# Splitting the value products of an fp32 attention into 64-row halves: four accumulator banks, scan units of 512 and a normalisation that goes through memory

## The reference

```python
# layer 0, for each image; w1 is 16 x 256
f = w1 @ xf + b1                       # 16 x N
energy = f.T @ f                       # N x N
attention = softmax(energy, axis=-1)
x2 = x + 0.1 * (xf @ attention.T)      # 256 x N
# layer 1: 3x3 convolution of sign(x2) with sign weights times a scale per channel,
# batch normalisation over all images, plus x2
```

## Time and profile before

| | |
|---|---|
| runs | 2257.96 us median of 3 (2257.39 to 2259.11) |
| profiled execution | 2258.62 us, its span 2256.8 us |
| granted TensorE clock, mean | 0.973 |
| busy PE, DVE, ACT, POOL | 95%, 71%, 59%, 36% |
| attention, about 85 to 2035 us | 512 groups |
| before it | projections and the first 24 scan units |
| after it | convolution to about 2203 us, then the final pass |

### The profile page before, as it was taken

The page is one execution under the profiler, slowest core; times in us unless marked ns, Lnnn a source line. Parts: engine busy times, 40 slices in busy tenths (PEclk is TensorE's granted clock), DMA queues, the critical chain, the costliest instruction groups (busy, mean ns, idle before and its releaser), DMA issues. The chain is left out here.

```text
span 2256.8 us, 26470 instructions
## 1 busy us (share of the span) xinstructions
PE 2145.6 (95%) x9152; PEld 1388.8 (62%) x9152; DVE 1613.0 (71%) x1719; ACT 1324.5 (59%) x1789; POOL 806.9 (36%) x664
## 2 busy tenths in 40 slices
PE   5799999999999999999999999999999999999990
PEld 2366666666666666666666666666666666664440
DVE  4677777777677777777677777777777777646778
ACT  3565566666656665666666566666666666652326
POOL 2433223334533333335433333335333333046760
PEclk7799999999999999999999999999999999999995
DMA  4110010011111100012111100011000001116008
GB/s 157 41 42 15 31 42 23 23 49 47 64 42 41 41 23 20 17 43 64 46 42 40 41 23 23 23 59 60 23 23 22 15 15 71 69 68 233 0 33 339
DMA packets 48632, 117.91 MB, mean 52 GB/s; under 512 B 6144, under 2 KB 7040, under 8 KB 48000
## 3 DMA queue, kind: packets, MB, share of 16 engines
q1 hardware_dynamic: 48512, 116.35, 14.8%
HBM read 76.22 MB, written 33.55 MB: 49 GB/s over the span
## 5 line engine op out<-in xcount | busy, mean ns | idle before, releaser
L520 DVE TENSOR_TENSOR Pl<-P,Ph 128x1024 fp32r<-128x1024 f32 x512 | 697.7, 1363 | 407.4 <-POOL Ph L635 359.8
L635 POOL CAST Ph<-P 128x1024 fp32r<-128x1024 f32 x480 | 503.8, 1050 | 1174.8 <-ACT P L434 1174.8
L347 PE MATMUL acc<-Ph,xh 128*128 128x512 f32 x2048 | 875.7, 428 | 0.0
L347 PE MATMUL acc<-Ph,xl 128*128 128x512 f32 x2048 | 805.8, 393 | 0.0
L434 ACT ACTIVATE P<-ee 128x1024 f32<-128x1024 f32 x512 | 525.1, 1026 | 420.1 <-PE ee L333 418.9
L444 ACT ACTIVATE sc<-sc,nb 128x1024 f32<-128x1024 f32 x512 | 557.5, 1089 | 255.9 <-DVE nb L510 255.2
L510 DVE TENSOR_REDUCE nb<-sc 128x1 f32<-128x1024 f32 x512 | 623.8, 1220 | 116.4 <-PE sc L341 116.0
L347 PE MATMUL acc<-Pl,xh 128*128 128x512 f32 x2048 | 637.1, 392 | 0.3
L347 PEld LDWEIGHTS acc<-Ph,xh 128*128 128x128 f32 x2048 | 385.2, 188 | 265.7 <-issue 195.4
L347 PEld LDWEIGHTS acc<-Pl,xh 128*128 128x128 f32 x2048 | 385.7, 188 | 88.5 <-DVE Pl L520 1.2
L347 PEld LDWEIGHTS acc<-Ph,xl 128*128 128x128 f32 x2048 | 386.6, 189 | 68.1 <-issue 5.7
(11 more groups left out here) (100 smaller groups left out, 823.5 us busy)
## 6 DMA issues: line engine op xcount, KB each, us to landing
wk<-xt SPq DMA_DIRECT2D x32, 512.0 KB, 3.6
xres<-x SPq DMA_DIRECT2D x32, 512.0 KB, 3.7
x<-xres SPq DMA_DIRECT2D x32, 512.0 KB, 2.7
xn<-x SPq DMA_DIRECT2D x16, 512.0 KB, 11.9
xr<-x SPq DMA_DIRECT2D x16, 512.0 KB, 10.2
out<-xr SPq DMA_DIRECT2D x16, 512.0 KB, 3.4
An<-x SPq DMA_DIRECT2D x14, 512.0 KB, 5.3
Bn<-x SPq DMA_DIRECT2D x12, 512.0 KB, 5.6
```

What stands on the lines that cost most here:

```text
L347: return pe.matmul(acc[c][:], w[:, m, c * 128:(c + 1) * 128], p[:, s, k * QC:(k + 1) * QC], start=first, stop=last)
L520: nc.vector.tensor_tensor(Pl[:, e % RP, :], P[:, e % 2, :], Ph[:, e % RP, :].bitcast(F32), ALU.subtract).then_inc(pl_done, 1)
L635: nc.gpsimd.tensor_copy(Ph[:, e % RP, :], P[:, e % 2, :]).then_inc(ph_done, 1)
```

## The change

1. Each attend becomes two matmuls of 64 rows, partitions 64 to 127 (`bot`) and 0 to 63 (`top`), into separate accumulators `acc_b[c]` and `acc_t[c]`: four banks in place of two.
2. `sc` shrinks to two tiles of one bank. Scan units are 512 wide, two per group (`SU` = 32 per tile), and a bank is reused one group later. Both scan units and both energies still stand together at the head.
3. VectorE's order becomes maximum, `lower(e - 1)`, maximum: `lower` is one group later and between the two maxima. ScalarE sums after each.
4. The transposition and spreading on TensorE go. VectorE transposes 32 x 32 blocks, SP issues four transfers into `U`, four into a buffer in memory, and one that loads it spread over all partitions into `R` (`load_r`, g = 4).
5. At the end of a tile ScalarE copies the bottom accumulator to `tb` and VectorE scales the top one; GpSimd's `add_x` is now a multiply, an add and an add for each c.
6. The rounding of xh for images 1 to 3 moves from ScalarE to GpSimd. `store_x2` moves from g = 3 to g = 4, and the exponential of the row statistics from g = 8 to g = 9.

```diff
+        acc_t = [ps(f"acct_{c}", [128, QC]) for c in range(CT)]
+        acc_b = [ps(f"accb_{c}", [128, QC]) for c in range(CT)]
-        sc = [ps(f"sc_{k}", [128, GW]) for k in range(2)]
+        sc = [ps(f"sc_{k}", [128, 512]) for k in range(2)]
...
+            def load_r(t):
+                sp.wait_ge(rd_out, 64 * (t + 1))
+                if t >= 1:
+                    sp.wait_ge(top_done, CT * t)
+                    sp.wait_ge(scaled, CT * t)
+                sp.dma_start(R[:], rd.rearrange("(o n) -> o n", o=1).to_broadcast([128, QC])).then_inc(r_in, 16)
...
+            def scan(v):
+                t, w = divmod(v, SU)
+                j, i = divmod(w, QT)
+                if v >= 2:
+                    pe.wait_ge(bsum_done, v - 1)
+                pe.matmul(sc[v % 2][:], U[t % 2][S0:S0 + KE, i * 128:(i + 1) * 128],
+                          T[t // CH % 2][S0:S0 + KE, j * 512:(j + 1) * 512], start=True, stop=True).then_inc(s_done, 1)
...
+            def attend(t, g, c, i, half):
+                k, w, p = ((0, xh, Ph), (0, xl, Ph), (1, xh, Ph), (1, xl, Ph), (0, xh, Pl), (1, xh, Pl))[i]
                 s = (t * G + g) % RP
+                rows = slice(half * 64, (half + 1) * 64)
+                to = (acc_t, acc_b)[half][c]
+                return pe.matmul(to[:], w[rows, g * GM + k, c * 128:(c + 1) * 128], p[rows, s, k * QC:(k + 1) * QC],
+                                 start=g == 0 and i == 0, stop=g == G - 1 and i == 5)
...
+                if 0 <= e < NG:
+                    energy(e, 0)
+                if u < NG:
+                    scan(2 * u)
+                if 0 <= e < NG:
+                    energy(e, 1).then_inc(e_done, 1)
+                if u < NG:
+                    scan(2 * u + 1)
...
+                        for i in range(6):
+                            if c == 0 and i == 4:
+                                pe.wait_ge(pl_done, n + 1)
+                            bot = attend(t, g, c, i, 1)
+                            top = attend(t, g, c, i, 0)
...
+                if g == 0 and t >= 1:
+                    copy_bottom(t - 1, 1)
                 if 0 <= e < NG:
                     exps(e)
                 if u < NG:
+                    block_sum(2 * u)
+                if g == G - 1 and t >= 0:
+                    copy_bottom(t, 0)
+                if u < NG:
+                    block_sum(2 * u + 1)
...
                 if g == 0 and t >= 1:
+                    scale_top(t - 1, 1)
                 if u < NG:
+                    block_max(2 * u)
+                if 0 <= e - 1 < NG:
+                    lower(e - 1)
                 if g == G - 1 and t >= 0:
+                    scale_top(t, 0)
+                if u < NG:
+                    block_max(2 * u + 1)
...
+                nc.gpsimd.tensor_tensor(tb[:, c, :], tb[:, c, :], R[:], ALU.mult).then_inc(scaled, 1)
+                pool.wait_ge(scaled, d)
+                pool.wait_ge(top_done, d)
+                nc.gpsimd.tensor_tensor(tb[:, c, :], tb[:, c, :], tc[:, c, :], ALU.add).then_inc(joined, 1)
+                pool.wait_ge(joined, d)
                 pool.wait_ge(xres_in[t % 2], 16 * (t // 2 + 1))
+                nc.gpsimd.tensor_tensor(xres[:, t % 2, c, :], tb[:, c, :], xres[:, t % 2, c, :],
                                         ALU.add).then_inc(x2_done, 1)
```

More of the change, by code:

```diff
@@ L115, in attention @@
         R = sb("R", [128, QC], F32)
[L116 to L124, removed]
+        tb = sb("tb", [128, CT, QC], F32)
+        sr = sb("sr", [128, 32], F32)
+        sh = sb("sh", [128, QT], F32R)
+        rows_t = sb("rows_t", [128, 32], F32)
+        nb = sb("nb", [128, 2, SU], F32)
+        bsum = sb("bsum", [128, 2, SU], F32)
+        dd = sb("dd", [128, SU], F32)
+        wg = sb("wg", [128, SU], F32)
+        wd = sb("wd", [128, SU], F32)
+        negm = sb("negm", [128, QT], F32)
         den = sb("den", [128, QT], F32)
@@ L285, in _ @@
                         load_xt(XG - 1)
-                    if g == 3 and t >= 1:
+                    if g == 4 and t >= 1:
                         store_x2(t - 1)
+                    if g == 4 and t >= 0:
+                        load_r(t)
                     if g == 5 and 0 <= t < NT - 1:
@@ L395, in _ @@
                         if g == 0 and t > 0:
-                            pe.wait_ge(evac_done, CT * (t - 1) + c + 1)
+                            pe.wait_ge(top_done, CT * (t - 1) + c + 1)
+                            pe.wait_ge(bot_done, CT * (t - 1) + c + 1)
                         if n == 0 and c == 0:
                             pe.wait_ge(fp_done, SL)
-                        for k in range(GM):
-                            attend(t, g, c, k, xh, Ph, g == 0 and k == 0, False)
-                            attend(t, g, c, k, xl, Ph, False, False)
@@ L402, in _ @@
[L402 to L415, removed]
@@ L437, in exps, with block_sum, copy_bottom @@
                 else:
-                    act.wait_ge(av_done, e - RP + 1)
+                    act.wait_ge(av_done, 2 * (e - RP + 1))
                     nc.scalar.activation(Ph[:, e % RP, :], ee[:], ACT.Exp).then_inc(p_done, 1)
[L441 to L445, removed]
+            def block_sum(v):
+                t, w = divmod(v, SU)
+                act.wait_ge(nmax_done, v + 1)
+                nc.scalar.activation(sc[v % 2][:], sc[v % 2][:], ACT.Exp, bias=nb[:, t % 2, w:w + 1],
+                                     accum_out=bsum[:, t % 2, w:w + 1]).then_inc(bsum_done, 1)
+            def copy_bottom(t, c):
+                if c == 0:
+                    act.wait_ge(acc_done, 2 * (t + 1))
+                else:
+                    act.wait_ge(av_done, 2 * G * (t + 1))
+                if t > 0:
+                    act.wait_ge(x2_done, CT * (t - 1) + c + 1)
+                nc.scalar.copy(tb[:, c, :], acc_b[c][:]).then_inc(bot_done, 1)
             def copy_f(s, bank):
@@ L539, in row_max @@
                 dve.wait_ge(negm_done, t + 1)
-                for j in range(UM):
-                    last = nc.vector.tensor_tensor(dd[:, j * QT:(j + 1) * QT], stp[:, 0:QT],
-                                                   nb[:, t % 2, j * QT:(j + 1) * QT], ALU.subtract)
-                last.then_inc(dd_done, 1)
+                nc.vector.tensor_copy(sh[:], negm[:]).then_inc(shift_h, 1)
+                nc.vector.tensor_tensor(dd[:].rearrange("p (j i) -> p j i", i=QT),
+                                        negm[:].rearrange("p (o i) -> p o i", o=1).to_broadcast([128, SL, QT]),
+                                        nb[:, t % 2, :].rearrange("p (j i) -> p j i", i=QT),
+                                        ALU.subtract).then_inc(dd_done, 1)
@@ L875, in _, with build @@
                                                sm[:, 7, c:c + 1], r, ALU.mult, ALU.add).then_inc(r_done, 1)
[L878 removed]
+def build(nc, x, xt, w1r, cols, wn, wt, gb, rd, x2d, out):
     with ExitStack() as ctx:
@@ L898, in build @@
         shared = (xn, An, Bn, fw, tab, wk, al, sems)
-        attention(nc, x, xt, w1r, cols, ident, wn, wt, x2d, T0, shared)
+        attention(nc, x, xt, w1r, cols, wn, wt, rd, x2d, T0, shared)
         convolution(nc, gb, x2d, out, shared)
```

178 lines of the change are left out of this document (68 added, 110 removed).

## The result

The changed kernel takes 2371.03 us (median of 4 runs, 2368.62 to 2375.5) against 2257.68 us before (4 runs): a ratio of 1.0509, 95% interval 1.0492 to 1.0527. It is slower by 5%. The profiled execution has a span of 2373.7 us, 116.9 more than before.

A forecast was written before the change was run, and what follows sets the result against it. The prediction took TensorE, busy 95%, to bound the kernel. Its terms, -107 - 48 + 162 + 26 + 41 + 8 + 5 + 8 = +95 on 2258.6, gave 2354 us; own range 2290 to 2410, for all 2215 to 2430.

The forecast's parts named there:

- the clock: TensorE after idle waits, as in g = 3 to 4: runs at its lower level for a while, +8 us (0 to 45).
- Term 1: TensorE's groups: 64-row pairs remove both borders, but the scan loop sets period 3.40 instead of 3.60; -107 us.
- Term 2: Stops at L414 in 32 tiles, extra border waits and L421 in 7 tiles disappear: -48 us.
- Term 3: End of a tile: six GpSimd operations and `lower` exclude each other, 5.5 us lost in 29.5 tiles; +162 us.
- Term 4: Row statistics at g = 9: `row_sum` waits for ScalarE and delays the next maximum, 0.85 us in 31 tiles; +26 us.
- Term 5: Split of x: GpSimd's rounding and subtraction collide with `lower`, 1.7 us for each of 24 pieces; +41 us.
- Small ones: Borders inside groups with 24 projections +8 us, scans before the attention +5, TensorE's clock +8.
- Faster, because `lower` gets its turn: At a tile's end `lower` runs between GpSimd's operations, costing 1.5 us a tile: -55 us, 2204 in all; chance 0.20.
- The clock falls in every tile: TensorE's clock drops in every tile and the loss stays on the path: 2400 us; chance 0.06.
- The halves run one after the other: TensorE's two 64-row attends do not overlap: +1395 us and more, 3650 in all; chance 0.02.
- A pair costs more: On TensorE a 64-row pair costs more than a full-height matmul, up to 0.33: about 2880 us; chance 0.09.

The follow-up runs named there:

- e1: Changed kernel with `lower` moved behind both maxima in VectorE's order: 2224.86 us, ratio to before 0.9864.
- e4: Changed kernel with attends 128 rows high again, into the top accumulator; the zeroed bottom one still copied and added: 2427.81 us.
- e10: e5 with attends 128 rows high, into the top accumulator; the zeroed bottom one still copied and added: 2282.27 us, ratio to before 1.0113.
- e2: Changed kernel with one GpSimd addition per channel half at a tile's end instead of three operations, bottom half left out of the result: 2237.81 us.
- e6: e5 with `lower` kept between the two maxima, as in the changed kernel: 2288.91 us.
- e8: Changed kernel with ScalarE's exponential of the row statistics ahead of its first sum at g = 9, not behind its second: 2355.79 us.
- e7: Changed kernel with GpSimd's rounding and subtraction of x for images 1 to 3 cut to 8 of 256 channels: 2325.14 us.
- e3: Changed kernel with the rounding of xh for images 1 to 3 back on ScalarE, subtraction still on GpSimd: 2368.25 us.
- e5: Changed kernel with `lower` behind both maxima and GpSimd's tile-end work cut to four operations, one per group: 2141.23 us, ratio to before 0.9495.

## Why the prediction was right

The forecast was 2354, slower, with the loop through the scan and GpSimd's work at the end of a tile as the reasons. Measured 2371, and both reasons hold. That the total came within 17 us is in part luck: the clock took some 37 us more than forecast, and smaller terms that were too large gave much of it back. By its own steps:

*Term 1, pairs and the loop (-107).* A pair costs 0.23 in the trace. The period was forecast at 3.40 from s' = h + 3.84 and h' = s + 2.96; it is 3.38 as a mean, alternating 3.20 and 3.56 to 3.61. The forecast had every second scan 0.4 late. In fact it is on time in one group and 0.6 late in the next; the two equations fix only the sum of two periods. The release, 1004.23 - 1000.44 = 3.79, was forecast as 3.74. e1 takes `lower` out of the loop and the period becomes 3.23; e4 and e10 bring the borders back and it becomes 3.60. In tile 31, without scans, the heads are 3.23 apart in place of 3.60: the two borders were worth 0.37 per group, not the 0.42 forecast.

*Term 2, stops removed (-48).* Not tested alone. It rests on the rows of before. Its larger waits stood at the images' borders, which is why the six border tiles took 369.6 there, 18 more than six ordinary ones.

*Term 3, the end of a tile (+162).* The six groups from the head of g = 15 (1003.64) to that of g = 5 (1030.56) take 26.92; forecast was 25.94. In the ordinary tiles and those with projections whose clock stayed up they take 25.1 to 25.5, so without the clock the loss per tile is 5.0 us, not 5.5. `lower` in g = 1, 2, 3 ends at 14.6 - 3.64 = 11.0, 15.4 and 21.0 after the head; forecast 10.8, 15.5, 21.3. That GpSimd and `lower` exclude each other both ways shows in their durations. e2 takes away four of the six operations and 133 us with them. That the order in which the two engines take turns does not matter was argued and not tested; the place of `lower` matters (e1), and so do the number and spacing of the operations (e6).

*Term 4, row statistics (+26).* It took 0.85 us per tile (its own figures, 4.75 less 3.86, give 0.89). At like clock e8 gives back 1.4 in an ordinary tile and 0.5 in one with projections, 0.9 on average over these 23; the small operations themselves stay in e8, so the term was not too large.

*Term 5, the split of x (+41).* Six border tiles take 414.9 against 6 x 61.75 = 370.5, 1.85 per piece, forecast 1.7; e7 takes away 46. But these six tiles have 15 of the stretches at the lower clock; against tiles without one (60.6), and at 1.55 for each stretch, about 1.2 per piece is the collision itself, an estimate, and the rest is the clock. And the forecast named the rounding moved to GpSimd along with the subtraction: e3 shows that on which engine the rounding runs makes no difference. The subtraction the kernel before had in the same place, where no loop through `lower` could feel it.

*Small ones.* Projections were forecast at +8 and are about -6: (64.8 - 61.75) / 2 = 1.5 each against 1.8 before, as the loop is waiting anyhow. The start was forecast at +5; up to tile 0's end it is +13, tile 0 itself included. The time after the last tile was missed. The convolution's first matmul waits longer, since GpSimd has six operations left:

```profile
2152.58 7.64 PE L824 MATMUL pm<-An,wk 128*128 128x512 bf16 x27 [8.43 <-DVE eps L831]
```

The wait was 3.30 before: +5.

The clock was the term most undersized. It was put at +8, with 45 as its upper bound, and 29 more stretches at about 1.55 make 45: the bound itself. They are 17 in g = 4, after the wait of 2.4 us that the forecast had foreseen, and most of the others around the split of x. No run held the clock up alone, but tiles with and without a stretch stand side by side in the one trace (5.54 and 7.07). The start and the end add another 13 to the forecast; the end of a tile without the clock, the split without the clock, and the projections give back 12 to 15 each. Of the 22 between the forecast's +95 and the +116.9 of the span, some 13 are then not assigned.

The forecast's own range has a slip: with terms 3 and 5 at their bounds one at a time it would be 2251 to 2412, not 2290 to 2410. The measured 2371 lies in both.

*The rivals.* "Faster, because `lower` gets its turn" failed: it had to cost under 2.3 us a tile and costs 5.0 before the clock is counted. "The clock falls in every tile" (2400, chance 0.06) came true in part: it fell in 17 of 28 and stayed on the path. "The halves run one after the other" failed with the pairs' 0.23. "A pair costs more" failed at 0.23. The Trainium skill ("TensorE: Matmul & The Clock Gate", Part 3, the measured speedups) gives 3.07 for four 32-row tiles. If its loss held for two 64-row tiles, a step would be 0.30, an estimate; the trace does not agree, it has 0.23.

## What to carry to other kernels

When a buffer is halved and reused one step earlier, write down the loop that now runs through it, engine by engine, with everything that stands in those queues between its members: here an unrelated subtraction of 1.14 us stood between two maxima, and moving it gave 146 us, the stretches at the lower clock that went with the waits included. Work that is moved onto an engine with a low busy share is not free if it comes in one piece: six GpSimd operations in two groups cost five microseconds a tile, four in four groups, with `lower` off the loop, almost nothing. Count what a repeated wait does to the clock as well: here that was over a third of the loss. Test such a change with its surroundings mended before giving it up: the pairs were worth 57 us in the kernel as changed, and 141 in the one that is 5% faster.

## What the runs showed of the hardware

Two TensorE borders between 64-row and 128-row work cost 0.37 us together, in fp32r and at the higher clock (3.60 against 3.23 per group, e10 and e5); 0.19 each if both cost the same.

GpSimd and a VectorE subtraction of two SBUF operands exclude each other nearly whole: 2.39 of subtraction on GpSimd makes a `lower` of 1.22 take 3.44, and a `lower` makes a rounding of 1.04 take up to 2.11. Maxima and scalings, which read PSUM, were never lengthened: all 1024 maxima of the changed kernel took 0.65 to 0.69, all 64 scalings 0.68 to 0.69. I had expected the first, from the rows of before, and only assumed the second.

Waits of TensorE as short as these can be followed by the lower clock, and the same wait need not be: after 2.4 us in g = 4 it fell in 17 of 28 tiles, in e1 after 1.30 us in 7. A whole stretch at the lower clock made such a group about 1.5 us longer.
